# First tile of the routed experts prepared inside the seventh sequence's attention

## The reference, cut to what matters

```python
k = apply_rope(x @ Wk.T); v = x @ Wv.T
q = apply_rope(einsum('btd,hkd->bhtk', x, Wq))          # two heads, one key and value head
w = softmax(where(causal, q k^T * scale, -inf))
s = (w @ v) @ Wo.T
# experts: 8, the best 2 of each token, 512 hidden features
y = gelu(x @ wg.T + wg_b)                                # exact gelu
h = y * (x @ w1.T + w1_b)
out = h @ w2.T + w2_b                                    # times the gate, summed over the two experts
```

## Time and profile before

| what | value |
|---|---|
| median of three runs | 531.67 us |
| profiled execution, its own time | 530.96 us |
| its span, first to last instruction | 529.1 us |
| TensorE matmul busy | 515.3 us, 97% |
| TensorE weight load busy | 387.3 us, 73% |
| VectorE busy | 389.5 us, 74% |
| ScalarE busy | 314.6 us, 59% |
| GpSimd busy | 234.8 us, 44% |
| up weight copies L1874, ScalarE | 71, mean 641 ns |
| turned tiles L1406, VectorE | 71, mean 311 ns |

### The profile page before, as it was taken

The page is one execution under the profiler, slowest core; times in us unless marked ns, Lnnn a source line. Parts: engine busy times, 40 slices in busy tenths (PEclk is TensorE's granted clock), DMA queues, the critical chain, the costliest instruction groups (busy, mean ns, idle before and its releaser), DMA issues. The chain is left out here.

```text
span 529.1 us, 12884 instructions
## 1 busy us (share of the span) xinstructions
PE 515.3 (97%) x3193; PEld 387.3 (73%) x3194; DVE 389.5 (74%) x1106; ACT 314.6 (59%) x830; POOL 234.8 (44%) x245
## 2 busy tenths in 40 slices
PE   9998999999998999999999999998999999999997
PEld 4856667767768999999999999976445545554544
DVE  6679778987785677767777777757788888788654
ACT  5636555455566666666666666667776667656511
POOL 4434766666521333333333333344476647523310
PEclk9999999999999999999999999999999999999999
DMA  8920133345445555656555556509100000000001
GB/s 236 387 99 11 42 105 107 100 113 171 161 41 105 141 141 146 152 144 151 146 149 147 148 135 161 131 27 284 34 1 21 0 20 22 20 0 22 20 12 30
DMA packets 85268, 54.01 MB, mean 102 GB/s; under 512 B 53088, under 2 KB 70016, under 8 KB 85104
## 3 DMA queue, kind: packets, MB, share of 16 engines
q1 hardware_dynamic: 80912, 44.66, 33.0%
q0 software_dynamic: 4320, 8.92, 4.7%
HBM read 37.82 MB, written 15.74 MB: 101 GB/s over the span
## 5 line engine op out<-in xcount | busy, mean ns | idle before, releaser
L637 POOL DMA_INDIRECT rows_y<-YO,W1E x71 | 68.8, 970 | 123.9 <-DVE YO L1400 121.4
L1881 ACT ACTIVATE AR<-bank,BGT 128x128 f32<-128x128 f32 x284 | 81.3, 368 | 69.9 <-PE bank L928 69.7
L1423 DVE SCALAR_TENSOR_TENSOR AR<-bank,B1T,AR 128x128 f32<-128x128 f32 x284 | 80.1, 344 | 5.1 <-ACT AR L1881 3.7
L601 POOL DMA_INDIRECT slots_x<-XR,SLOT x64 | 63.8, 997 | 32.8 <-DMA slots_x<-XR,SLOT 15.8
L928 PE MATMUL bank<-AR,WGE 128*128 128x128 f32 x568 | 75.3, 276 | 1.7 <-DVE AR L1406 1.7
L946 PE MATMUL bank<-W2E,AR 128*128 x568 | 75.1, 275 | 0.5 <-DVE AR L1423 0.5
L937 PE MATMUL bank<-AR,WGE 128*128 128x128 f32 x568 | 75.0, 275 | 0.0
L928 PEld LDWEIGHTS bank<-AR,WGE 128*128 128x128 f32 x568 | 69.1, 192 | 2.0 <-issue 1.8
L946 PEld LDWEIGHTS bank<-W2E,AR 128*128 128x128 f32 x568 | 69.1, 192 | 0.7 <-issue 0.7
L937 PEld LDWEIGHTS bank<-AR,WGE 128*128 128x128 f32 x568 | 69.1, 192 | 0.0
L1800 ACT ACTIVATE AR<-bank,AR 128x512 f32<-128x512 f32 (+1 forms) x64 | 33.8, 528 | 54.5 <-DVE AR L1330 54.4
(11 more groups left out here) (216 smaller groups left out, 911.4 us busy)
## 6 DMA issues: line engine op xcount, KB each, us to landing
WGE<-in_wgu SPq DMA_DIRECT2D x71, 256.0 KB
XG<-slots_x SPq DMA_DIRECT2D x140, 32.0 KB
slots_x<-W1E SPq DMA_DIRECT2D x7, 585.0 KB, 7.5
X<-in_x SPq DMA_DIRECT2D x8, 256.0 KB, 5.6
SPARE<-in_wgu SPq DMA_DIRECT2D x8, 256.0 KB
W2E<-in_w SPq DMA_DIRECT2D x8, 256.0 KB
XR<-rows_y SPq DMA_DIRECT2D x8, 256.0 KB, 5.2
XNT<-rows_y SPq DMA_DIRECT2D x8, 256.0 KB, 5.4
```

Source lines behind the costliest of these rows:

```text
L601: pool.indirect_dma_start(out=slots_x, out_offset=bass.IndirectOffsetOnAxis(ap=SLOT[:, k, n:n + 1], axis=0), in_=XR[:, n, :], in_offset=No ...
L637: pool.indirect_dma_start(out=rows_y, out_offset=bass.IndirectOffsetOnAxis(ap=DST[:, j:j + 1], axis=0), in_=YO[q % 2][:], in_offset=None). ...
L1423: s = dve.scalar_tensor_tensor(out=HT[u][:, c, :], in0=B[3 + u][:, c * P:(c + 1) * P], scalar=B1T[:, bass.ds(e, 1), c], in1=ZB[u][:, c, :] ...
L1881: act.activation(ZB[u][:, c, :], B[1 + u][:, c * P:(c + 1) * P], ACT.Gelu, bias=BGT[:, bass.ds(e, 1), c]).then_inc(c_gelu, 1)
```

## The change

The change touches only the passage from the seventh sequence's attention to the experts. VectorE turns tile 0 in `finish(6)`, behind the last reciprocal and ahead of the last two `combine`. ScalarE copies the up weights of tiles 0 and 1 in `attend(6)`, ahead of the exponentials of steps 6 and 7, each behind a register load. The copy of sequence 7's values goes from the end of `attend(6)` into `finish(6)`, behind the last `turned` and ahead of `head0`. TensorE's block of waits ahead of tile 0 is cut to `proj_free`; the wait for the loads stands ahead of the first down product and the wait for `o_done` ahead of the second one. VectorE and ScalarE lose their waits for `pv_done` and `o_done`.

```diff
 # TensorE, c_step
                 if not (isinstance(j, int) and j < 1):
+                    if isinstance(j, int) and j == 1:
+                        pe.wait_ge(ld_moe, 16 * N_MOE)
+                    if isinstance(j, int) and j == 2:
+                        pe.wait_ge(o_done, TPS * NB)
                     pe.reg_load(e_down, TEXP[0:1, bass.ds(j - 1, 1)])
                     c_down(j - 1, 1 - u, pe.snap(e_down, min_val=0, max_val=E - 1))
...
-            pe.wait_ge(ld_moe, 16 * N_MOE)
-            pe.wait_ge(exp_done, NS * NB)
-            pe.wait_ge(pt_done, NS * NB)
-            pe.wait_ge(o_done, TPS * NB)
             pe.wait_ge(proj_free, 4 * (NB + 1))
 # VectorE
             def finish(b):
                 denominator(b, NS - 1)
+                if b == NB - 1:
+                    c_turn(0, 0)
                 combine(b, 2)
                 combine(b, 3)
...
             dve.wait_ge(ld_moe, 16 * N_MOE)
-            dve.wait_ge(pv_done, NS * NB)
-            dve.wait_ge(o_done, TPS * NB)
             dve.wait_ge(r_texp, 1)
             dve.reg_load(e_this, TEXP[0:1, 0:1])
             dve.reg_mov(e_last, e_this)
-            c_turn(0, 0)
 # ScalarE
+            def first_up_weights(j, register):
+                act.wait_ge(ld_moe, 16 * N_MOE)
+                act.wait_ge(r_texp, 1)
+                act.reg_load(register, TEXP[0:1, j:j + 1])
+                c_up_weights(j, j, act.snap(register, min_val=0, max_val=E - 1))
...
+                    if b == NB - 1 and k == 6:
+                        first_up_weights(0, e_this)
+                    if b == NB - 1 and k == 7:
+                        first_up_weights(1, e_next)
                     exponent(b, k)
...
-                if not last:
+                if not last and b != NB - 1:
                     values(b + 1, 1 - u)
...
                 turned(b, NS - 1)
+                if b == NB - 1:
+                    values(b + 1, 1 - b % 2)
                 head0(b, 3)
                 bring_table(ACT.Gelu if b < NSEQ - 1 else ACT.Silu)
...
             def c_step(j, q, last=False):
-                if not last:
+                if not last and not (isinstance(j, int) and j == 0):
                     act.reg_load(e_next, TEXP[0:1, bass.ds(j + 1, 1)])
...
-            act.wait_ge(ld_moe, 16 * N_MOE)
-            act.wait_ge(pv_done, NS * NB)
-            act.wait_ge(o_done, TPS * NB)
-            act.wait_ge(r_texp, 1)
-            act.reg_load(e_this, TEXP[0:1, 0:1])
-            c_up_weights(0, 0, act.snap(e_this, min_val=0, max_val=E - 1))
```

More of the change, by code:

```diff
@@ L1371, in finish, with c_turn @@
                 denominator(b, NS - 1)
+                if b == NB - 1:
+                    c_turn(0, 0)
                 combine(b, 2)
                 combine(b, 3)
+            def c_turn(j, q):
+                dve.wait_ge(c_ld[q // 2], (j - q) * 16 + 64)
+                if not (isinstance(j, int) and j < 2):
+                    dve.wait_ge(c_h, j - 1)
+                dve.transpose(XT[q % 2], XG[q // 2][:, (q % 2) * P:(q % 2 + 1) * P]).then_inc(c_xt, 1)
             dve.wait_ge(ld_attn, 16 * N_ATTN)
@@ L1400, in c_out @@
                 dve.tensor_scalar(YO[u][:], YB[u][:], TAGS[:, bass.ds(j, 1), 1], None, ALU.mult).then_inc(c_yo, 1)
[L1402 to L1406, removed]
             e_next, e_this, e_last = (dve.alloc_register(f"dve_expert_{n}") for n in ("next", "this", "last"))
@@ L1818, in head0, with c_up_weights @@
                 act.activation(O0[c], reg, ACT.Copy, scale=RD[:, k:k + 1]).then_inc(o0_done, 1)
+            e_next, e_this = (act.alloc_register(f"act_expert_{n}") for n in ("next", "this"))
+            def c_up_weights(j, u, e):
+                if not (isinstance(j, int) and j < 2):
+                    act.wait_ge(c_h, j - 1)
+                act.activation(WU[:, u:u + 1, :], SPARE[:, bass.ds(e, 1), :], ACT.Copy).then_inc(c_wu, 1)
+            def first_up_weights(j, register):
[3 more added lines that the diff above has]
+                c_up_weights(j, j, act.snap(register, min_val=0, max_val=E - 1))
             def attend(b, u, first=False, last=False):
@@ L1868, in _ @@
             finish(NB - 1)
[L1871 to L1874, removed]
             def c_gelu_of(j, u, e):
@@ L1882, in c_gelu_of @@
                                    bias=BGT[:, bass.ds(e, 1), c]).then_inc(c_gelu, 1)
-            e_next, e_this = (act.alloc_register(f"act_expert_{n}") for n in ("next", "this"))
             def c_step(j, q, last=False):
                 e = act.snap(e_this, min_val=0, max_val=E - 1)
-                if not last:
+                if not last and not (isinstance(j, int) and j == 0):
                     act.reg_load(e_next, TEXP[0:1, bass.ds(j + 1, 1)])
```

## The result

The changed kernel took 529.38 us (median of 20 executions, 528.48 to 531.35), the kernel before 531.37 us (20 executions beside it). The ratio is 0.9968, with a 95% interval of 0.9956 to 0.9981: 1.7 us faster, 1.0 to 2.3, and within the 0.5% that were called no change. The medians themselves lie 1.99 apart. The prediction was 530.1 us and a gain of 1.6. Executions of one kernel lie 1 to 2 us apart, much of it with the mean granted clock: the changed kernel's 13 executions at 0.999 and above have a median of 529.01 us, the seven at 0.997 lie between 530.21 and 530.53. A few executions are disturbed by some 7 us, which the ratios leave out.

What follows compares the result with a forecast made beforehand. TensorE, busy 97% of the span, bounds the kernel, with 2.31 us of idle time to win. Expert start -1.68 plus tile 1's turning +0.05 gives -1.63, rounded to -1.6: 530.1 us from 531.67, range 528.7 to 531.9.

Steps and rivals of the forecast that it cites:

- ScalarE's tail, 0.28 late: End of attention: `turned` now ahead of the values' copy makes `head0` and the last `weigh` 0.28 us later.
- TensorE's first products: Start of the experts: first gate product 1.60 us earlier, tile 1's gate product 1.68 us earlier.
- Tile 0's turning, hidden: VectorE, between last reciprocal and `combine`: turning takes 0.31 us, hidden in a 1.21 us hole, cost nothing.
- Tile 1's register loads: VectorE behind the last `combine`: loads needn't wait for its end, tile 1 is turned just in time, cost 0.05 us.
- The rival with 0.4: VectorE's register load waits for `combine`: tile 1's gate product 0.4 us late, gain 1.2, 530.5 us; chance 0.09.
- The copies: ScalarE's two up weight copies ahead of steps 6 and 7's exponentials: hidden in 1.24 and 1.01 us holes, cost 0.
- The gelu table: ScalarE behind `head0`: load 1.28 us plus a dummy, ready at 160.32, 0.37 us to spare before the first gelu.
- The rival of the drain: Gelu set usable 1.38 us later, first down product 0.45 late: gain 1.2, 530.5 us; chance 0.02.
- The shift is carried whole: TensorE runs without a gap through the next 170 us, so the -1.6 us reaches the end in full.
- the gain given back: Rival, later in the kernel: a transfer keeping its own time takes the gain away, 531.7 us; chance 0.08.
- The signs: Profile after: `head0` 0.28 us later, gate product within 0.5 of `weigh`, step 7's exponential to end changed by 1.6.
- uncovered copies: Rival: ScalarE's loads or copies don't fit ahead of steps 6 and 7's exponentials, +0.7, 532.3 us; chance 0.06.

Runs made afterwards that it cites:

- e3: VectorE's and TensorE's parts of the change alone, on the kernel before: 531.42 us, ratio 0.9991 to the kernel before.
- e5: Changed kernel with tile 0 turned behind the last two `combine` instead of ahead: 530.44 us, ratio 0.9995 to the kernel before.
- e6: Changed kernel with TensorE's old block of four waits put back ahead of tile 0: 530.44 us, ratio 0.9985 to the kernel before.
- e1: Changed kernel with the copy of sequence 7's values put back ahead of the last `turned`: 529.46 us, ratio 0.9989 to the kernel before.
- e12: Changed kernel with `head0` ahead of the last `turned` and the values' copy shared by ScalarE and VectorE: 566.76 us on another, slower-clocked chip, no ratio.
- e7: Changed kernel with two more copies ahead of step 7's exponential, three instead of one: 529.63 us, ratio 0.9963 to the kernel before.
- e2_head_first: Changed kernel with the values' copy split, half ahead of the last `turned`, half behind `head0`: 528.11 us, ratio 0.9940 to the kernel before.
- e11_idle_waits: Changed kernel with two already met TensorE waits put back ahead of tile 0: 579.07 us on another, slower-clocked chip, ratio 1.0217.
- e4: ScalarE's part of the change alone, TensorE and VectorE as in the kernel before: 534.16 us, ratio 1.0024 to the kernel before.

## Why the prediction was right

The total was 0.7 us under the forecast, 0.3 of it because the kernel before came out at 531.37 with 20 executions where three had given 531.67. The gain was 1.7 us by the ratio where 1.6 was said. That it comes so near is in part luck: beside the passage's -1.51 the two profiles differ by -0.21 in the attention, -0.33 in the loop and +0.35 behind it, none of them forecast, and these cancel to -0.19. Step by step, in distances from the mark (the forecast's times less 156.77):

- *What bounds.* Confirmed by e3, e5 and e6: tile 0's turning, TensorE's `o_done` and the up weights each would hold the passage if left in place. At tile 2's gate the turning put back costs 0.94 us and TensorE's waits 0.90; ScalarE's whole part put back costs 0.86, the 0.34 won by its old order already taken off.
- *ScalarE's tail, 0.28 late.* Measured 0.33, and e1 shows that it is the values' copy: 0.34.
- *TensorE's first products.* Forecast: weigh 2.18, gate 0 2.63, gate 1 4.41, tile 2's gate 7.14 (with the 0.05 of tile 1's turning). Measured 2.23, 2.75, 4.53, 7.26. The 0.12 are the tail's 0.05 and a `weigh` that took 0.52 to the next group, not 0.45: it is 0.52 behind a wait, and 0.45 in no profile but that of e12, where `weigh` doesn't wait. The forecast was right that the gate product's 0.97 behind a gap becomes 0.89 without one. It called the array cold in the first case; the granted clock was 1.00 there, so this isn't the lower clock, and what else it is no run shows.
- *Tile 0's turning, hidden.* Right in cost, wrong in the size of its cover: I took the rows to land at 154.5, the lower end, and in this execution they landed at 158.4, where the reciprocal had ended at 157.7. The landing itself was near the 2.2 us that I took (158.4 - 156.69 = 1.7 behind the last issue); the start of the issues was not. It stood between 149.7 and 154.9 in the first ten profiles. The step held since a late turning has room until the `combine` and the gate product behind it start.
- *Tile 1's register loads.* The case without a wait for `combine` came true: turned 1.10 us after `combine` began (1.03 forecast, and less than 1.1 was the sign), no wait before gate 1; its group took 0.94 us in place of 0.89, the 0.05 of the sum. The rival with 0.4 is out.
- *The copies.* Free, with 0.73 and 0.50 us left. e7 shows that this is the cover, and all of it.
- *The gelu table.* The rival of the drain is out. The forecast had the gelu set usable 1.28 us plus a short dummy after the load starts; in e2_head_first the first gelu starts 1.41 us after it, 0.11 behind the dummy. The Trainium skill (ScalarE: Activation LUTs, What ACT_TABLE_LOAD costs) has 1.28 us for the load, which the row agrees with, and some 2.66 us for a switch to another set in all, which this measurement speaks against: from the end of the copy ahead of the load (157.85) to the first gelu (159.28) 1.43 us pass, and the measurement decides.
- *The sum.* -1.63 forecast, -1.51 measured to tile 2's gate. Not forecast: 0.33 more inside the loop, because the profile before had a late store at tile 7. I had read the loop as fully busy and didn't look at its rate. Whether that part is the change's stays open (see e11_idle_waits).
- *The shift is carried whole.* Through the experts it is, with that 0.33 on top. Behind the scores of sequence 8 the changed kernel's profile is 0.35 us longer than that of the kernel before, at L1050. The forecast had the gain given back as a rival with all of it lost; a fifth may be.
- *The signs.* `head0` ends 0.33 us later behind the start of step 7's exponential (2.78 against 2.45), where 0.28 was said. The gate product follows `weigh` after 0.52 where at most 0.5 was said. The distance from that exponential to the end changed by 1.49 us (373.04 to 371.55), where 1.6 was said and anything else was to count as wrong; taken as strictly as that, this sign fails by 0.1.

The case named as slower, uncovered copies, didn't come. The one kernel of this family that ended slower than the kernel before (e4) had its copies covered: it lost 0.33 us by the values' copy and, in its profile, more by the clock, which the forecast didn't have.

## What to carry to other kernels

Where a bounding engine idles at a hand-over, list every chain that ends there: here three (`o_done` at 159.7, the turned tile at 160.9, the first up weights at 161.2 in the kernel before) ended within 1.5 us of one another, and taking away one gives the difference to the next, not the idle time. Put small preparations where the other engine waits, measure the hole (0.50 us left here), and look at what the new order makes wait: the copy moved here cost a third of a microsecond, which splitting it gave back twice over. To judge a fraction of a microsecond, measure from a mark close by on the bounding engine; over 8 us it repeats to 0.02 us where the totals scatter by 1 to 2.

## What the runs showed of the hardware that was not expected

- The granted clock fell to the lower level (0.50, 1.2 GHz) for about 3.4 us in e4_copies_alone, after TensorE had idled 0.99 and then 1.65 us, and cost 1.6 us; after 0.66 and 1.65 in the kernel before it stayed at 1.00. It fell there again at 369.6, after 1.82 us of idle time. But in e3_turn_alone TensorE idled 1.74 us at the same place (up to 367.08) and the clock stayed at 1.00. So idle time ahead of a fall was seen, and that it is the cause was not shown.
- The clock also fell at 24 to 28 us in the profiles of the changed kernel and of e3_turn_alone (0.59 and 0.55 in the first), and in none of the other twelve. There TensorE had been busy 9.97 of the 10 us before. The first scores start at 34.65 and 34.71 us in these two and at 32.98 to 33.56 in the others.
- A register load on VectorE starts 0.1 us after the instruction ahead has started (160.7 behind the `combine` of 160.60), long before it ends at 160.95.
